# Message passing in four graph layers: ScalarE fetches every 64th tile of the pair pass by one-row transfers

## What is computed

```python
h = relu(layernorm(x)); x = x + gcn(h, W1, W2)      # two gathers and sums: h[src], summed by dst
h = relu(layernorm(x)); x = x + neighbour_norm(h)   # one gather and sum
h = relu(layernorm(x)); x = x + weighted_gcn(h, ew) # one gather and sum, weighted
# the last layer, with h = relu(layernorm(x))
hihj = concatenate([h[src], h[dst]], axis=-1)       # a pair of rows per edge
e = exp(silu(bn(hihj @ Wf + bf)));  we = node_vec1[src] * e
z = silu(bn(einsum('ed,hdk->ehk', hihj, Wg) + bg))  # bn: mean and variance over all edges
out = x + bn(segment_sum(we / sum_we[dst] * z, dst))
```

## Time and profile before

| what | us |
|---|---|
| median of 3 runs | 14196.12 (14173.72 to 14206.94) |
| profiled execution, first to last instruction | 11157.3 |
| its own time with what lies around the span | not given |
| POOL busy | 8098.3 (73% of the span) |
| PE / DVE / ACT busy | 4270.1 / 3430.3 / 3212.6 |
| pair pass, first to last gather | 8394.5 to 10366.1 |

### The profile page before, as it was taken

The page is one execution under the profiler, slowest core; times in us unless marked ns, Lnnn a source line. Parts: engine busy times, 40 slices in busy tenths (PEclk is TensorE's granted clock), DMA queues, the critical chain, the costliest instruction groups (busy, mean ns, idle before and its releaser), DMA issues. The chain is left out here.

```text
span 11157.3 us, 112702 instructions
## 1 busy us (share of the span) xinstructions
PE 4270.1 (38%) x19462; PEld 2948.2 (26%) x19462; DVE 3430.3 (31%) x7386; ACT 3212.6 (29%) x7261; POOL 8098.3 (73%) x8241
## 2 busy tenths in 40 slices
PE   1222222342222233333333433343464333443687
PEld 0111111121111112111111333333353333333576
DVE  4000001110001112000001422222245677777898
ACT  3333333343333334333333300000031111111465
POOL 4777777657777775777777677777766777777676
PEclk5555555665555555555555555556675555555899
DMA  4333333233333333333333222222214555555444
GB/s 105 81 81 81 81 81 81 76 88 81 81 81 81 81 81 102 81 81 81 81 81 81 59 54 54 54 54 54 54 48 148 159 162 163 166 166 170 149 167 134
DMA packets 702798, 1071.72 MB, mean 96 GB/s; under 512 B 164740, under 2 KB 547065, under 8 KB 675209
## 3 DMA queue, kind: packets, MB, share of 16 engines
q0 software_dynamic: 323616, 664.87, 23.0%
q10 hardware_dynamic: 247712, 225.10, 6.1%
q1 hardware_dynamic: 130793, 174.77, 4.9%
HBM read 904.67 MB, written 161.05 MB: 96 GB/s over the span
## 5 line engine op out<-in xcount | busy, mean ns | idle before, releaser
L460 POOL DMA_INDIRECT big<-table_parts,tile_cols x4596 | 4348.0, 946 | 1563.2 <-issue 1400.2
L641 PE MATMUL psum<-big 128*128 x4992 | 1722.0, 505 | 3998.4 <-SPq L472 3044.2
L641 PEld LDWEIGHTS psum<-big 128*128 128x128 bf16 x4992 | 670.0, 141 | 4980.6 <-issue 2814.6
L460 POOL DMA_INDIRECT big<-ptable,tile_cols x1563 | 1496.6, 957 | 498.4 <-issue 476.0
L460 POOL DMA_INDIRECT big<-table,tile_cols x1532 | 1454.6, 949 | 469.5 <-issue 467.0
L596 ACT ACTIVATE big<-big,ones 128x2048 bf16<-128x2048 bf16 x312 | 624.4, 2001 | 3573.5 <-PE psum L641 2381.1
L589 ACT ACTIVATE big<-iota_col,dl_tab 128x128 bf16<-128x128 f32 x4992 | 1490.7, 387 | 32.9 <-PEq L765 12.5
L1656 PE MATMUL psum<-acc,big 128*128 x3328 | 785.0, 419 | 1205.5 <-DVE big L1632 1193.4
L618 DVE TENSOR_REDUCE acc<-psum 128x128 f32<-128x384 f32 (+1 forms) x196 | 109.7, 560 | 3558.1 <-PE psum L644 1783.4
L713 PE MATMUL psum<-big 128*128 x3328 | 754.6, 419 | 1158.3 <-SPq L472 619.7
L1656 PEld LDWEIGHTS psum<-acc,big 128*128 128x128 f32 x3328 | 701.8, 315 | 1288.5 <-issue 1288.2
(11 more groups left out here) (301 smaller groups left out, 4278.8 us busy)
## 6 DMA issues: line engine op xcount, KB each, us to landing
big<-table_parts SPq DMA_DIRECT2D x11904, 0.8 KB
big<-dl_rows ACTq DMA_DIRECT2D x104, 1024.0 KB
zrows<-big ACTq DMA_DIRECT2D x104, 1024.0 KB, 5.5
big<-zrows SPq DMA_DIRECT2D x104, 1024.0 KB, 4.9
big<-table_parts,tile_cols POOLq DMA_INDIRECT x4596
big<-table SPq DMA_DIRECT2D x3968, 0.5 KB
table_parts<-big SPq DMA_DIRECT2D x42, 672.0 KB, 3.5
big<-ptable,tile_cols POOLq DMA_INDIRECT x1563
```

The costliest lines, as they stand in the source:

```text
L460: pool.indirect_dma_start(out=slots[:, t % (groups * GT), 0:width], out_offset=None, in_=tab, in_offset=bass.IndirectOffsetOnAxis(ap=idx_t ...
L641: last = nc.tensor.matmul(held, m, rows_t, start=False, stop=False, skip_group_check=True)
```

## The change

In pass 4 POOL leaves out tile 127 and every 64th tile after it, up to tile 1535. That is 23 tiles of 1563. ACT fetches their rows by one-row transfers of 520 bytes, 128 to a tile, in four halves: 32 row addresses are loaded into registers behind the half's two copies, 16 rows are issued ahead of the half's squares and 16 behind them. In all there are 92 register loads and 2944 one-row transfers. The rows don't go into the ring but into four places of their own in `big`, and each place has a semaphore that SP waits on before it calls the group landed. Tile 127's rows are fetched in halves 0 to 3, tile 191's in halves 4 to 7, and so on. DVE reads every item's rows by an offset from the table, and the setup now adds to the offset for the items of these tiles (four DVE operations, three of them with a wait for the operation itself, two POOL tables and one more small load on SP). Semaphores of other blocks are merged to make room, with the numbers waited for changed to match.

```diff
+PAIR_FIRST, PAIR_EVERY, PAIR_AHEAD = 127, 64, 79
+PAIR_PLACES = 4
...
+        pair_place = big[:, PAIR_AT:PAIR_AT + PAIR_PLACES * ACW].rearrange("p (u f) -> p u f", f=ACW)
...
             for g in range(TGROUPS):
                 if g >= groups:
                     pool.wait_ge(s_free, freed + g - groups + 1)
-                for k in range(tiles_of(g) - has_side(no, g)):
+                for k in range(tiles_of(g) - left_out(no, g)):
...
+                k = pair_tile_of(no, g)
+                if k is not None:
+                    sp.wait_ge(s_pair[k % PAIR_PLACES], 16 * P)
+                    sp.sem_clear(s_pair[k % PAIR_PLACES])
                 sp.sem_inc(s_landed[no], 1)
...
+            def fetch(act, q, part):
+                k, j = (q - first) // PAIR_HALVES, 2 * ((q - first) % PAIR_HALVES) + part
+                if not 0 <= k < len(PAIR):
+                    return
+                for e in range(j * P // (2 * PAIR_HALVES), (j + 1) * P // (2 * PAIR_HALVES)):
+                    if e % SIDE_LOAD == 0:
+                        numbers.clear()
+                        words = [nc.alloc_registers(f"pair{no}_{k}_{e + i}", engines=[act.engine]) for i in range(SIDE_LOAD)]
+                        nc.regs_load(words, pair_of[k:k + 1, e:e + SIDE_LOAD])
...
+                    at = numbers[e % SIDE_LOAD] // size
+                    act.dma_start(pair_place[e:e + 1, k % PAIR_PLACES, :], flat[:, bass.ds(at, width)]).then_inc(s_pair[k % PAIR_PLACES], 16)
...
-                dve.wait_ge(s_last, 64)
+                dve.wait_ge(s_last, 80)
+                nc.vector.tensor_scalar(pair_of, pair_of, 4 * ACW, None, ALU.mult)
...
+                step(nc.vector.tensor_tensor(pair_hit, tile_f.unsqueeze(2).to_broadcast([P, IG, NPAIR]),
+                                             pair_tile.unsqueeze(1).to_broadcast([P, IG, NPAIR]), ALU.is_equal))
+                step(nc.vector.tensor_tensor(pair_hit, pair_hit, pair_move.unsqueeze(1).to_broadcast([P, IG, NPAIR]), ALU.mult))
+                step(nc.vector.tensor_reduce(pair_slot, pair_hit, AX.X, ALU.add))
+                nc.vector.tensor_tensor(slot_at, slot_at, pair_slot, ALU.add)
...
                     nc.scalar.copy(weight_tab[:, q * HALF:(q + 1) * HALF], zbuf[:, h, :, SCW]).then_inc(s_scores, 1)
+                    fetch_pair(act, q, 0)
                     act.wait_ge(s_zout[h], 16 * (q // 2 + 1))
                     act.wait_ge(s_summed, 2 * q + 1)
                     z = zbuf[:, h, :, 0:F]
                     nc.scalar.activation(z, z, ACT.Square).then_inc(s_squared, 1)
+                    fetch_pair(act, q, 1)
```

More of the change, by code:

```diff
@@ L83, in gnn_kernel @@
     assert SIDE_FIRST == RGROUPS and RGROUPS - SIDE_EVERY == LEAD and SIDE_BASE + len(SIDE) * SIDE_SPAN <= E
+    PAIR = list(range(PAIR_FIRST, NT - GT, PAIR_EVERY))
+    PAIR_HALVES = PAIR_EVERY // HALF
+    NPAIR = -(-len(PAIR) // PAIR_PLACES) * PAIR_PLACES
+    assert PAIR_FIRST % GT == GT - 1 and PAIR_EVERY % HALF == 0 and PAIR_FIRST + PAIR_EVERY * NPAIR > NT and len(PAIR) <= 32
+    assert PAIR_AHEAD <= PAIR_FIRST - (PAIR_HALVES - 1) * HALF
+    assert PAIR_AHEAD + (PAIR_HALVES - 1) * HALF + HALF - 1 + NW <= PAIR_PLACES * PAIR_EVERY + HALF
     CHUNKS = NW // CW
@@ L332, in gnn_kernel @@
         no_dst = work[0:BODY, 0, 2 * F:3 * F]
+        pair_at = work_flat[:, 4 * CC:]
+        pair_hit = pair_at[:, 0:IG * NPAIR].rearrange("p (g k) -> p g k", k=NPAIR)
+        pair_tile, pair_move = (pair_at[:, IG * NPAIR + k * NPAIR:IG * NPAIR + (k + 1) * NPAIR] for k in range(2))
+        pair_slot = pair_at[:, IG * NPAIR + 2 * NPAIR:IG * NPAIR + 2 * NPAIR + IG]
+        assert PAIR_EVERY % SLOTS == 0 and IG * NPAIR + 2 * NPAIR + IG <= WB - 4 * CC
         found = ring_flat[:, 0:2 * CC].rearrange("p (b k f) -> p b k f", b=2, f=F)
@@ L445, in has_side, with pair_tile_of, left_out @@
             return no < PASSES - 1 and g in SIDE
+        s_pair = [sem(f"pair_rows{k}") for k in range(PAIR_PLACES)]
+        def pair_tile_of(no, g):
+            t = g * GT + GT - 1
+            return PAIR.index(t) if no == PASSES - 1 and t in PAIR else None
+        def left_out(no, g):
+            return has_side(no, g) or pair_tile_of(no, g) is not None
         def landed_count(no, g):
-            return 16 * sum(tiles_of(k) - has_side(n, k) for n in range(no + 1)
+            return 16 * sum(tiles_of(k) - left_out(n, k) for n in range(no + 1)
                             for k in range(g % RGROUPS, g + 1 if n == no else TGROUPS, RGROUPS))
@@ L506, in fetch, with pair_rows @@
                     sp.dma_start(slots[e:e + 1, t % RSLOTS, 0:width], flat[:, bass.ds(at, width)]).then_inc(s_side, 16)
+            return fetch
+        def pair_rows(no, tab, width, row_bytes):
+            flat, size = tab.rearrange("n f -> (n f)").unsqueeze(0), row_bytes // width
+            numbers = []
+            first = (PAIR_FIRST - PAIR_AHEAD) // HALF - (PAIR_HALVES - 1)
+            def fetch(act, q, part):
[7 more added lines that the diff above has]
+                        nc.regs_load(words, pair_of[k:k + 1, e:e + SIDE_LOAD])
+                        numbers.extend(nc.snap(word, engines=[act.engine], donate=True, min_val=0, max_val=(N - 1) * row_bytes,
+                                               guaranteed_mod_val=0, out_of_modulus=row_bytes) for word in words)
+                    at = numbers[e % SIDE_LOAD] // size
+                    act.dma_start(pair_place[e:e + 1, k % PAIR_PLACES, :], flat[:, bass.ds(at, width)]).then_inc(s_pair[k % PAIR_PLACES], 16)
             return fetch
@@ L788, in _ @@
                 nc.gpsimd.iota(tile_last, [[GT * P, RG]], base=GT - 1, channel_multiplier=GT, **kw)
+                nc.gpsimd.iota(pair_tile, [[PAIR_EVERY, NPAIR]], base=PAIR_FIRST, channel_multiplier=0, **kw)
+                for k in range(PAIR_PLACES):
+                    nc.gpsimd.memset(pair_move[:, k::PAIR_PLACES], float(PAIR_AT + (k - PAIR_FIRST % SLOTS) * ACW))
                 nc.gpsimd.iota(wplus1[:, 0:NW], [[1, NW]], base=1, channel_multiplier=0, **kw).then_inc(s_const, 1)
@@ L835, in _ @@
                     sp.dma_start(to, side_src).then_inc(s_last, 16)
+                span = PAIR_EVERY * P
+                pair_src = src[PAIR_FIRST * P - span + P:][0:len(PAIR) * span].rearrange("(k s) -> k s", s=span)[:, span - P:]
+                sp.dma_start(pair_of, pair_src).then_inc(s_last, 16)
                 sp.wait_ge(s_pad, 4)
@@ L1631, in _ @@
                             dve.wait_ge(s_prod, items0 + n + Z_GROUP)
-                        last = nc.vector.scalar_tensor_tensor(zbuf[:, h, u, 0:ACW], dyn(ring_flat, slots[u], ACW), in_win[:, h, u:u + 1],
+                        last = nc.vector.scalar_tensor_tensor(zbuf[:, h, u, 0:ACW], dyn(big[:], slots[u], ACW), in_win[:, h, u:u + 1],
                                                               bank[n % Z_BANKS][:, 0:ACW], ALU.mult, ALU.add)
@@ L1665, in load_dst @@
                                   ).then_inc(s_dl, 16)
+                fetch_pair = pair_rows(no, ptable, ACW, 4 * ACW)
                 load_dst(0)
@@ L1686, in _ @@
                 act.wait_ge(s_dl, 16 * HALVES)
-        s_v, s_root, s_wide, s_exp, s_sums = (sem(n) for n in ("bn_steps", "bn_root", "bn_wide", "bn_silu_and_exp", "bn_sums"))
+        s_v, s_wide, s_exp, s_sums = (sem(n) for n in ("totals_steps", "bn_wide", "bn_silu_and_exp", "bn_sums"))
         mean, var, scale_r, shift_r = (rows[:, k, :] for k in (RT0, RT1, RT2, RT3))
@@ L1697, in gnn_kernel @@
         s_col, sq_col = (work_flat[:, NI + k:NI + k + 1] for k in range(2))
+        BN_STEPS = 17
         with nc.Block() as block:
@@ L1869, in _ @@
                                          start=False, stop=False, skip_group_check=True).then_inc(s_prod, 1)
-        s_v, s_ones, s_h, s_gram, s_stats, s_root, s_wide, s_shift, s_shifted, s_scaled, s_out = (sem(n) for n in (
-            "end_steps", "end_ones", "end_h", "end_gram", "end_stats", "end_root", "end_wide", "end_shift", "end_x_shifted",
+        s_ones, s_h, s_gram, s_stats, s_wide, s_shift, s_shifted, s_scaled, s_out = (sem(n) for n in (
+            "end_ones", "end_h", "end_gram", "end_stats", "end_wide", "end_shift", "end_x_shifted",
             "end_scaled", "end_out"))
```

32 lines of the change are left out of this document (17 added, 15 removed).

## The result

| | us |
|---|---|
| kernel before, median of 4 runs | 14194.99 (14173.72 to 14206.94) |
| changed kernel, median of 4 runs | 14525.95 (14496.17 to 14578.91) |
| ratio, 95% interval | 1.0245 [1.0226, 1.0263] |
| profiled execution of the changed kernel, time and span | 14578.91 and 14576.8 |

A forecast was written before the change was run, and what follows sets the result against it. POOL's gathers were taken to bound the pair pass, with ACT's extra work covered. Removed gathers -28.9 and setup +0.4 gave -28.5 us, so 14196.1 became 14168 us (-0.20%), range 14140 to 14204.

The forecast's parts named there:

- the half of ACT: Pair pass, ACT: copies, register load, 32 rows and the rest take 13.6 us of a 19.07 us half; costed at nothing.
- ACT becomes the bound: Rival, pair pass: at 0.61 us per row ACT needs 22.9 us a half, +352 us, 14548; chance 0.05.
- I let it stand as a constant: Whole kernel: the 3039 us between profiled span and median of the runs were taken as unchanged.
- squares: ACT, each half: rows ahead move the squares by 0.3 us, done 5.0 us before DVE reads them.
- Removed gathers, -28.9: Pair pass, POOL: 23 gathers fewer at 1.249 to 1.262 us each save 28.9 us.
- POOL sets the pace: Pair pass: POOL issues a gather every 1.262 us, none inside the pass waiting for a free place.
- Setup, +0.4: Setup: added DVE work and a small load cost 0 to 2.5 us, taken as 0.4.
- End-node numbers: ACT's load queued behind the rows goes out later, yet lands 3.4 us before DVE wants it.
- Register load, 2.1 us: ACT: loading 32 registers costs 2.1 us, as on SP and PE, whose rows spoke against the skill's 6.4 us.
- The rival of instructions that cost more outside the profile: Rival, whole kernel: about 5980 added instructions at 0.027 us each add 161 us, giving 14329; chance 0.04.
- Gathers dearer: Rival: each gather costs 0.395 us more in unprofiled executions, so 38 us are saved, 14159; chance 0.13.
- landings later: Rival, pair pass: data land later and a third to two thirds of the gain goes, 14182; chance 0.15.

## Why the prediction was wrong

**The step that failed is the half of ACT, "13.6 us of a half", and with it "covered, and costed at nothing".** Measured, it is 27.1 us: 0.66 us a row instead of 0.32, which is 32 x 0.34 = 10.9 us more, and a register load some 2.4 us dearer: 13.6 + 13.3 = 26.9. The cover was larger than taken too, about 23.7 us a half in ordinary executions instead of 19.07, since everything was slower. The same as a difference of two traces: stores 2780.9 us from first to last in the changed kernel run again, against 2440.4 with blocks of 16 rows on the same chip, +340. The profiled execution of it took 14547.27, which is 345 more than the 14202.37 of before.

```profile
L1744 ACTq DMA_DIRECT2D zrows<-big x104: 2/542/1414, 10990.6 to 13771.5; - x104
```

```profile
L1744 ACTq DMA_DIRECT2D zrows<-big x104: 520/521/612, 11011.0 to 13451.4; - x104
```

**The rival "ACT becomes the bound" is what happened**, by its mechanism and nearly by its number: 14548 from 0.61 us a row, deciding from 0.48. I gave it 0.05. The price of 0.61 was a bound by another kind of transfer, and the real reason was another, the slow stretches. That the number came so near is luck: the rival had 22.9 us a half where 27.1 were measured, and a cover of 19.07 where there were about 23.7, and the two errors cancel. But the bound did its work: its upper end lay above the point where the rival decides, and this should have brought the range up to it.

**"I let it stand as a constant" failed first.** The profile's span and the median differed by 3039 us, 21%. This was a sign that the profiled execution wasn't like the timed ones, and that durations in it could be too short. Those of POOL's gathers were not (median 0.944 us there and 0.945 in the profile taken again), those of the queues were. All three stretches of reasoning that call something hidden (squares, end-node numbers, ACT as a whole) took durations from it. Against it stood the statement that nothing in the trace shows what fills the rest; that was true and should have counted against the forecast, not for it.

**Removed gathers, -28.9:** taken alone they gave -23 us (-37 to -7), which fits. In the changed kernel no gain can be seen, because POOL waited for places.

**"POOL sets the pace":** true of the trace shown, not of the timed executions. There POOL waits 3181.9 us for SP over the whole kernel before, and 642.0 of it in the pair pass.

```profile
POOL big L460 <- SPq L483: 3181.9, 549, 19.1
```

**Setup, +0.4:** too small to test. The first gather of pass 0 starts at 280.2 us where it did at 278.6, +1.6, inside the 0 to 2.5; but in the variants with the longer setup it starts anywhere from 277.8 to 280.7.

**End-node numbers, "3.4 us to spare":** gone. It is the wait that the chain goes through, 444.5 us in 70 halves. DVE waited for squares 5 times, 5.0 us in all, so the other part of that step held; the delay was in the same queue, one instruction later.

**Register load, 2.1 us:** the traces give 4.63 in its place on ACT, and 2.165 behind the end-node load; mine was below the one that mattered. The Trainium skill ("Runtime: NRT & Kernel Launch", on instruction fetch mechanics) has about 200 ns per register, for loads from HBM; for 32 that makes an estimate of 6.4 us. Here the numbers come from a table on the chip, and the estimate is above both medians. "The rows speak against it" held for SP and PE, and I had no row of ACT in that place.

**The rival of instructions that cost more outside the profile** (0.027 us each, 14329) had the right kind of thing at a sixth of the size. On ACT, the rows' 5888 instructions took 1929 us where 942 were counted, 0.17 us more each. **Gathers dearer** and **landings later** are not what happened: gathers have the same duration, and the same packets by blocks of 16 rows cost nothing. Because of the levels the part of 141 to 143 us that two increments or a fixed-address transfer per row seem to cost isn't settled; for the whole change the full queue is shown by the moved register load, by half the rows and by blocks of 16.

## What to carry to other kernels

Compare the profiled span with the median first: if they are far apart (here 3039 us, where ordinary executions have 2), the profile is of another kind of execution, durations in it can be too short, and a cover that rests on them isn't one until the profile is taken again. Count the instructions of a queue and not only its transfers, since each of thousands of small ones can cost 0.3 us in the mean, where a register move by itself is 29 ns; 184 transfers of 16 rows cost nothing that could be measured, 2944 of one row by register addresses cost 331 us. When the upper bound of an unknown price lies past the point from which a rival decides, that rival belongs in the range.

## What the hardware showed that I had not expected

- A queue that issues many small instructions falls into stretches in which each takes about 0.7 or 1.4 us: register moves of 29 ns in the median, and increments of 17 ns, alike. 90 rows in 60.16 us on SP, 16 rows in 20.96 on ACT.
- The same kernel had one execution of 11157.3 us, while all of its timed runs in five comparisons took 14160 to 14396.
- Loading 32 registers took 4.63 us on ACT behind a 1 MB store and two copies, and 2.165 or 1.31 behind the load of end-node numbers. When the load stood elsewhere, the first row behind the store took 1.76 us and not 0.47.
- Without SP's 15872 one-row transfers (four passes of 3968) the kernel before is 1320 to 1370 us faster, although POOL then issues 124 gathers more.
